# Leaving out TensorE's unread products in the two later attentions of a two-layer perceiver kernel

## The reference

```python
x = x + _L0_xattn_ref(_layernorm(x), ctx, ...)
x = x + _L0_attn_ref(_layernorm(x), ...)
x = x + _L0_ffn_ref(_layernorm(x), ...)
x = x + _L1_xattn_ref(_layernorm(x), ctx, ...)
x = x + _L1_attn_ref(_layernorm(x), ...)
x = x + _L1_ffn_ref(_layernorm(x), ...)
```

## Time and profile before

| what | value |
|---|---|
| median of 3 runs | 872.93 us (870.93 to 876.23) |
| the profiled execution: its own time | 877.42 us |
| the profiled execution: its span | 875.6 us |
| mean granted TensorE clock | 0.91 |
| TensorE products busy | 809.4 us (92%), 6020 instructions |
| TensorE weight loads busy | 636.2 us (73%) |
| VectorE busy | 587.3 us (67%) |
| ScalarE busy | 452.9 us (52%) |
| GpSimd busy | 359.9 us (41%) |

### The profile page before, as it was taken

The page is one execution under the profiler, slowest core; times in us unless marked ns, Lnnn a source line. Parts: engine busy times, 40 slices in busy tenths (PEclk is TensorE's granted clock), DMA queues, the critical chain, the costliest instruction groups (busy, mean ns, idle before and its releaser), DMA issues.

```text
span 875.6 us, 16465 instructions
## 1 busy us (share of the span) xinstructions
PE 809.4 (92%) x6020; PEld 636.2 (73%) x6020; DVE 587.3 (67%) x890; ACT 452.9 (52%) x979; POOL 359.9 (41%) x401
## 2 busy tenths in 40 slices
PE   8889998899999799999979999888997999999997
PEld 7523335688888588687658888767885788888886
DVE  5989985787878577797756665566774455455453
ACT  2878885344544345354545666424553445444543
POOL 2288886332422344355801112213332445444442
PEclk9855555999999999998989999998999999999999
DMA  5189996022111122111201111101110233332331
GB/s 176 42 152 161 177 174 127 25 61 79 56 54 57 49 73 90 38 47 55 61 1 37 38 43 43 61 25 49 50 38 25 73 91 96 88 104 83 101 91 49
DMA packets 107066, 64.35 MB, mean 73 GB/s; under 512 B 71921, under 2 KB 94961, under 8 KB 106994
## 3 DMA queue, kind: packets, MB, share of 16 engines
q1 hardware_dynamic: 106994, 63.37, 29.0%
HBM read 46.05 MB, written 0.52 MB: 53 GB/s over the span
## 4 chain that ended last, share of the span: by engine, by line
PE 60%; DVE 16%; POOL 9%; issue 6%; ACT 5%; DMA 2%; SPq 1%; DVEq 0%; POOLq 0%; ACTq 0%
PE ps L159 16%; PE ps L160 14%; PE ps L161 14%; POOL pt L780 6%; PE ps L1636 3%; DVE x L1404 2%; PE ps L1962 2%; PE ps L1112 2%; PE ps L1616 2%; POOL nb L787 1%; DVE qrot L2129 1%; DVE u_lo L1878 1%; PE ps L1123 1%; DVE qodd L2112 1%; ACT h_hi L1388 1%
## 5 line engine op out<-in xcount | busy, mean ns | idle before, releaser
L294 POOL TENSOR_TENSOR wa_lo<-raw,wa_hi 128x512 fp32r<-128x512 f32 (+1 forms) x120 | 143.6, 1200 | 190.8 <-ACT wa_hi L283 190.4
L294 POOL TENSOR_TENSOR wb_lo<-raw,wb_hi 128x256 fp32r<-128x256 f32 (+1 forms) x112 | 95.7, 855 | 236.8 <-ACT wb_hi L283 236.8
L159 PE MATMUL ps<-xt_hi,wa_hi 128*128 128x512 f32 (+1 forms) x348 | 139.2, 400 | 3.9 <-DVE lg L1333 3.0
L160 PE MATMUL ps<-xt_lo,wa_hi 128*128 128x512 f32 (+1 forms) x348 | 135.1, 388 | 0.0
L161 PE MATMUL ps<-xt_hi,wa_lo 128*128 128x512 f32 (+1 forms) x348 | 134.6, 387 | 0.0
L1398 DVE TENSOR_TENSOR h_lo<-hh,h_hi 128x512 fp32r<-128x512 f32 x56 | 61.8, 1103 | 48.3 <-ACT h_hi L1388 48.3
L283 ACT ACTIVATE wa_hi<-raw 128x512 fp32r<-128x512 f32 (+1 forms) x120 | 64.7, 549 | 53.8 <-PE ps L161 30.0
L883 ACT ACTIVATE kres<-ps,nb,qs 128x1024 int16<-128x1024 f32 x64 | 77.0, 1204 | 17.9 <-POOL nb L787 15.8
L1016 DVE TENSOR_REDUCE nm<-ps 128x1 f32<-128x1024 f32 x64 | 78.0, 1222 | 9.9 <-PE ps L706 7.6
L1396 DVE TENSOR_TENSOR hh<-sg,ps 128x512 f32<-128x512 f32 x56 | 38.5, 687 | 65.2 <-PE ps L161 61.0
L159 PEld LDWEIGHTS ps<-xt_hi,wa_hi 128*128 128x128 f32 x348 | 66.8, 192 | 16.8 <-issue 5.0
(11 more groups left out here) (307 smaller groups left out, 1860.1 us busy)
## 6 DMA issues: line engine op xcount, KB each, us to landing
raw<-w_l1f SPq DMA_DIRECT2D x44, 256.0 KB, 2.7
raw<-w_l1f SPq DMA_DIRECT2D x44, 128.0 KB, 2.0
raw<-w_l0a SPq DMA_DIRECT2D x16, 256.0 KB, 2.7
raw<-w_l1p SPq DMA_DIRECT2D x32, 128.0 KB, 2.1
raw<-w_l1x SPq DMA_DIRECT2D x32, 128.0 KB, 2.2
raw<-w_l1a SPq DMA_DIRECT2D x16, 256.0 KB, 2.5
raw<-w_l0f SPq DMA_DIRECT2D x12, 256.0 KB, 2.7
raw<-w_l0a SPq DMA_DIRECT2D x16, 128.0 KB, 2.1
```

The lines of the kernel that those rows point to most:

```text
L159: nc.tensor.matmul(o, a[0], b[0], start=start, stop=False, **kw)
L160: nc.tensor.matmul(o, a[0], b[1], start=False, stop=False, **kw)
L294: last = nc.gpsimd.tensor_tensor(split_lo, src, split_hi.bitcast(F32), ALU.subtract)
```

## The change

The calls of `busy` in `l1x_pe` and in `l1a_pe` are taken out: 14 and 3 products in step n = -2 of the cross-attention, and 2, 4, 6 and 3 in the self-attention, 32 in all. No other instruction, no semaphore and no wait changes. The calls inside `ln_pe` stay, in the self-attention (`idle=(3, 0, 2, 2)`) as elsewhere, and so does the call in the first cross-attention.

```diff
@@ pair_step of l1x_pe
                 some(out_x, 2 * n, 0)
-                if n == -2:
-                    busy(pe, 4, 14)
                 some(turn_x, 2 * n + 4, 0)
                 if within(2 * n + 2):
                     mix_ctx(pe, n + 1, 1)
-                if n == -2:
-                    busy(pe, 4, 3)
                 some(key_scores, 2 * n + 6, 0)
@@ l1a_pe
             l1a_tables(pe)
-            busy(pe, 3, 2)
             pe.wait_ge(x_ready, 8)
             y_start(R_PB)
             ln_pe(pe, 4, idle=(3, 0, 2, 2))
@@
             last.then_inc(la["lt"], 1)
-            busy(pe, 2, 4)
             pe.wait_ge(la["lte"], 2)
             pe.wait_ge(la["krot"], 1)
@@
                 if j >= 2:
                     for a in range(2):
                         l1a_out(pe, j - 2, j % 2, a)
-                if j == 0:
-                    busy(pe, 2, 6)
                 if j == STEPS - 1:
                     l1a_out(pe, j - 1, 0, 0)
-                    busy(pe, 2, 3)
                 l1a_turn(pe, j, j % 2)
```

## The result

The changed kernel takes 878.61 us (median of 4 runs, 877.53 to 880.13) against 871.93 for the kernel before (4 runs, 870.87 to 876.23). The ratio is 1.0073, interval 1.0038 to 1.0108: slower by 6.7 us by the medians and 6.4 by the ratio, with 3.3 and 9.4 as the ends. The time lies inside the stated range and the change has the sign of the sum; the median is under 1%, the upper end of the interval a little over it.

A forecast was written before the change was run, and what follows sets the result against it. It took TensorE's waits, mostly for VectorE and ScalarE, and its varying clock as the bound. Terms -0.1 - 0.7 + 1.6 + 1.6 + 2.3 = +4.7 us on the 872.93 median gave 877.6 us, range 869.5 to 884.

The forecast's parts named there:

- the sum: All gains and losses over the whole kernel added up: +4.7 us, slower by 0.5%.
- What covers the removed products: At most of the six calls VectorE or ScalarE releases what follows, so removal gains little; 0.8 us in all.
- The first idle time: TensorE idle before the cross-attention's first transposes: about 4 us, 1.15 plus the 14 removed products.
- the three behind the first transposes: Cross-attention: the scores behind them wait for ScalarE's copy, so removal gains 0.1 us, bounds 0 and 0.65.
- the three of the last step: Self-attention: on the path at half clock, costing 1.31 us; removal gains 0.7 us, bounds 0 and 1.3.
- The fall in the cross-attention: Clock falls behind the emptied wait, slowing first transposes and scores: +1.6 us, bounds 0 and 3.1.
- The falls in the self-attention: Clock falls at first scores, +1.6 us (0 to 2.3), and from step 0 to step 1, +2.3 (0 to 3.4).
- The rule on the cold penalty: Skill's rule, throttled time times one minus 1.2/2.4: 3.4 us from self-attention step 0 to 1, where the prediction took 2.3.
- A: Rival: the clock holds at the emptied places, leaving only gains of 0.8 to 1.4 us; about 871.8 us; chance 0.19.
- B: Rival: cold stretches at the three places reach their upper ends, 8.8 us, no last-step gain; 881.7 us; chance 0.11.
- C: Rival: from the self-attention's first scores one fall does not end; two such steps give +9.8, 882.7 us; chance 0.07.
- D: Rival: present clock dips vanish as later work moves, new ones fail to come; -4.7, 868.2 us; chance 0.05.

The follow-up runs named there:

- x_only: Only the 14 and 3 unread products of the cross-attention left out of the kernel before; ratio 1.0054, interval 1.0028 to 1.0080.
- last_only: Only the 3 unread products ahead of the self-attention's last transposes left out of the kernel before; ratio 1.0012, interval 0.9985 to 1.0040.
- scores_only: Only the 4 unread products ahead of the self-attention's first scores left out of the kernel before; ratio 1.0031, interval 1.0003 to 1.0059.
- x14_only: Only the 14 unread products ahead of the cross-attention's first transposes left out of the kernel before; one run, no ratio given.
- narrow: Kernel before with each unread product of 512 columns at all six places replaced by four of 8 columns; ratio 1.0054, interval 1.0024 to 1.0083.
- fill_late: Kernel before plus 8 unread products in cross-attention, 7 in self-attention step 1, 10 replacing the last step's 3; ratios 0.9978 and, repeated, 0.9966.

## Why the prediction was right, and where its terms were off

**What covers the removed products.** Right for five of the six calls: what they stood ahead of was released by VectorE or ScalarE. The idle times of 2.4 and 2.6 us are as worked out, and the three behind the first transposes gave 0.0 us at full clock (predicted 0.1). The first idle time was 5.5 us and not about 4, because the prediction added the 14 products to a wait that had been shortened by scores at half clock. Only the three of the last step were on the path. That term was 0.7; measured 0.24 in the pair of profiles, since the half clock went on to 668 instead of ending near 664.7, and 0.7 on the average of the profiles that fall there.

**The fall in the cross-attention.** Predicted +1.6, with 3.1 as its upper end if the half clock reached the context product. In the changed kernel it did, and it took the second transposes along, which I had not counted: +3.5 there, 1.5 given back later in this execution, X +2.1. In x_only it did not, and the counted pieces plus the second transposes came to +1.8. This is the term most undersized. Over all profiles X is 17.97 on average with the 14 in place and no fill added (seven: 18.44, 18.33, 16.91, 18.34, 18.37, 18.52, 16.90) and 20.32 without (20.56, 19.86, 20.55): +2.35. The spread of the seven is the later fall, which is there in five and not in two.

**The falls in the self-attention.** Predicted +1.6 and +2.3; the spacings grew by 1.4 and 1.8. In the second, mask to third projection product took 2.3 us longer (5.16 against 2.90 by the timelines), as predicted. The six products that VectorE waits for ended later still: its rotation of the queries started 6.61 us behind the mask of step 1, against 4.02 before, 2.6 us later. But 0.8 came back, since VectorE's weights took 0.69 us there and 1.45 before. Its timeline in the changed kernel, and before:

```profile
593.79 1.28 DVE L2103 SCALAR_TENSOR_TENSOR qrot<-ps,parts,tab 128x1024 f32<-128x1024 f32 x1 [1.45 <-PE ps L161]
596.58 0.69 DVE L2141 TENSOR_TENSOR soft<-soft,rc 128x512 f32<-128x512 f32 x1
```

```profile
592.14 1.28 DVE L2112 SCALAR_TENSOR_TENSOR qrot<-ps,parts,tab 128x1024 f32<-128x1024 f32 x1 [0.68 <-PE ps L161]
594.93 1.45 DVE L2150 TENSOR_TENSOR soft<-soft,rc 128x512 f32<-128x512 f32 x1
```

Why the weights took less is open. S is 21.49 on average with the products (20.97, 22.50, 20.96, 20.97, 22.52, 20.99) and 23.99 without (24.18, 23.80): +2.5, less than the 3.9 of the sum. The two spacings were sized 0.7 too high, and with the products in place the clock falls there too in two profiles of six, which adds 0.5 to their side; and what the second place adds once the first is empty is next to nothing (23.75 and 23.80).

**The sum.** 2.35 + 2.5 - 0.7 = 4.2 us by stretches, against 4.7 predicted and 6.7 (3.3 to 9.4) measured. The agreement of the sums is partly luck: one term was too small and one too large. The 2.5 us above are inside the interval and I have no stretch to put them in. The time of 878.61 us is only 1.0 above the forecast of 877.6, because the kernel before came out 1.0 lower than in the runs that the forecast started from.

**A sentence that fell.** "Wherever TensorE was idle for 1.9 to 2.3 us in this part, the clock fell" was true of that one profile. (Of the steps called full speed beside it, show one; the next is already slow, behind the 1.89 us.) The same wait of 2.34 us is followed by full clock in the changed kernel (first stretches above, 456.6 to 459.9), and last_only went through its 2.65 us wait at full clock. Its timeline, and its stretch behind the wait:

```profile
651.73 0.35 PE L159 MATMUL ps<-wb_hi,ot_hi 128*128 128x256 f32 x1 [2.65 <-POOL wb_lo L294]
```

```profile
651.80:656.00 4.20, 3.42 (x34) 3.09 (x35) 0.00 (x0) 1.31 (x3) 0.94 (x1) 1.00 0.10 31
```

Behind the wait of 2.34 us the clock fell in seven of the eleven profiles that leave it bare. Ahead of the first transposes, where the prediction saw 1.15 us left idle, it was 2.36 us in seven of the ten profiles with the 14 products, as in scores_only:

```profile
441.22 0.66 PE L1623 MATMUL ps<-ident,soft 128*128 128x128 f32 x4 [2.36 <-DVE soft L1874]
```

All ten had these transposes at full clock, 0.66 us. Behind an idle time of 4.0 to 5.5 us they were at half clock in all four profiles that had it (changed, x_only, x14_only, narrow). So the same length of idle time came out differently at different places, and the length alone does not tell whether the clock falls.

**The rule on the cold penalty.** The Trainium skill, "TensorE: Matmul & The Clock Gate", HAM oscillation, would charge half of the 6.6 us from 586.3 to 592.9, 3.3 us; VectorE started 2.6 us later, and the spacing grew by 1.8. For X it would charge half of 13.5 us, 6.8, where the delayed pieces add up to 3.5. TensorE was busy for 5.72 of the 6.6 us and 8.09 of the 13.5. (The prediction's own comparison, 3.4 against 2.3, was not like with like: 3.4 is for the whole stretch of 6.7 us, 2.3 for 5.3 us of it.) The measurement decides: here, where TensorE waits inside the cold stretch and another engine can make up time behind it, the rule gives an upper bound.

**The rivals.** A (the clock holds) is out: the clock fell behind each of the three emptied places. B's upper end came true in X only, in the changed kernel (+3.5 in the delayed pieces); three of the rule's charges of 3.4 would have been 10.2, more than its 8.8. C did not come: behind each stretch the clock returned. D happened, in both directions, as scatter.

## What to carry to other kernels

Products that nobody reads can be worth their place: before taking them out, look at what releases the next real instruction (if it comes later, they cost nothing) and at the clock behind the idle time that would open. A piece of the chain of waits is not yet a gain: 0.65 us on the chain gave 0.0 when removed at full clock, because a copy ended in the same instant. And where single falls of the clock, worth 1.5 to 2.6 us each, come and go from run to run, one pair of profiles can hide a loss of 6.7 us; compare fixed stretches over several profiles.

## What the runs showed of the hardware

The same instructions behind the same idle times got full clock in one execution and 0.50 in another: X of 16.9 or 18.3 to 18.5 with the same work, and S of 21.0 or 22.5 with the same self-attention. The single runs of the kernel before spread accordingly, from 867.12 to 877.48 us in one session of 35. Unread products need not fill a lull wholly: with 0.9 to 2.36 us left idle ahead of the first transposes the clock held in ten profiles of ten, and with 0.27 us left in step 1 of the self-attention it held in fill_late.
